# Three edits ahead of the main loop of a gated state-space layer: fp8 rounding by a step from the exponent bits, absolute maxima in one pass, the last gate store issued from the loop

## The chip, the cores and the metric

The program runs on one core of one Trainium2 chip. The metric is the device time of one execution in microseconds (us), the median of several runs. Engines are named PE (matrix unit), DVE (vector), ACT (scalar), POOL and SP (which here only issues transfers).

## The reference

x is 4 sequences of 1024 tokens of width 128. It is normalised (layernorm), run through a recurrent layer with 32 heads (`s`), and multiplied by a gate that comes from an fp8-rounded linear layer. What matters here is the gate:

```python
amax = jnp.max(jnp.abs(t))
scale = 448.0 / jnp.maximum(amax, 1e-12)
q = (t * scale).astype(jnp.float8_e4m3fn).astype(jnp.float32)
...
xq, wq = fake_quant_fp8(xn), fake_quant_fp8(weight)
g = silu(einsum('bsd,od->bso', xq, wq) + bias)
out = x + s * g
```

The largest absolute value is taken over the whole of x (and over the whole weight), so no token can be rounded before all are normalised.

## The kernel before

There are two parts, each a block of five instruction streams (one per engine) with semaphores between them. `prepare` does what is needed once: layernorm, transposes of the weights, cumulated angles and decays, and the gates. `units` then loops over 8 groups of 512 tokens (`t`, NS = 8) and 8 groups of 4 heads (`q`). No engine begins `units` before all have ended `prepare`. The order on each engine is the order of the code.

In `prepare`, tokens lie on the free axis of `xnT` (128 x 4096). DVE takes the largest and the smallest value of each quarter of it (`extreme`, L589). PE turns the result (L459), DVE makes the scales `sc` from it (L662 to L667), and ACT writes, for each t, the scaled numbers `fv` and their absolute values `fmag` (`gate_input`, L833). DVE rounds them in five passes over 512 columns (`quantise`, L687 to L693): fp8 by conversion at half size, a rounding by adding and taking off a large number for small values, and a choice between the two. PE multiplies the result with the rounded weight (L515) on top of the bias (`gate_bias`, L507). ACT applies Silu (L899) into `fgate`, a buffer of two halves, and SP stores that to DRAM (L270), the last step of `prepare` for it: it then waits until all gate stores have landed.

Between these steps of the gates, others are woven in: `log_part` on ACT (L888) with a subtraction on DVE (L737), and at t = 4 and 5 transposes on PE (L531), copies on ACT (L904) and after t = 5 three stores by SP (L274). `gate_input(t + 2)` waits until DVE has rounded t, Silu of t waits for PE, and from t = 2 on for the store of t - 2. `carry` belongs to `units`: its second half is first written at t = 1 of the loop.

Of the kernel before, what the change touches and what calls it, by code (L numbers as in the profile page):

```python
# [22 lines left out]
FP8 = mybir.dt.float8e4  # L23
# [4 lines left out]
P = 128  # L28
# [28 lines left out]
FP8_MAX = 448.0  # L57

# [32 lines left out]
def prepare(nc, K, dram, scratch, cum_stored, logs_stored, bc_loaded, xn_loaded):  # L91
# [3 lines left out]
    with ExitStack() as ctx:  # L95
# [49 lines left out]
        am, am2, sc = sb("a_am", [P, 2]), sb("a_am2", [2, 3]), sb("a_sc", [P, 7])  # L145
# [3 lines left out]
        half = sb("a_half", [P, ST], FP8)  # L149
        xq = sb("a_xq", [P, 2, ST], BF16)  # L150
        by_two = lambda a: tmp[:, a * ST:(a + 2) * ST].rearrange("p (i t) -> p i t", i=2)
        fv, fmag, fgate, small = by_two(0), by_two(2), by_two(4), tmp[:, 6 * ST:7 * ST]
# [31 lines left out]
        gate_stored = [sem("a_gate_stored0"), sem("a_gate_stored1")]  # L184
# [4 lines left out]
        def _(sp):  # L189
# [78 lines left out]
            for t in range(NS):  # L268
# [9 lines left out]
            for i in range(2):  # L278
                sp.wait_ge(gate_stored[i], 16 * NS // 2)
# [255 lines left out]
        def _(dve):  # L535
# [49 lines left out]
            peak = st32[:, 5, 0:2 * BATCH].rearrange("p (b i) -> p i b", i=2)  # L585

            def extreme(b, op):
                i = 0 if op == ALU.max else 1
                link(nc.vector.tensor_reduce(peak[:, i, b:b + 1], xnT[:, b * L:(b + 1) * L], AX.X, op))  # L589

            for g in range(0, 8, 2):
                dve.wait_ge(bc_squared, g + 1)
                nc.vector.tensor_copy(big[:, 512 * g:512 * g + 512], ps[B_BANK[g]][:]).then_inc(bc_copied_v, 1)
                extreme(g // 2, ALU.max)
# [23 lines left out]
            for i in range(BATCH):  # L618
# [8 lines left out]
            extreme(0, ALU.min)  # L627
            extreme(1, ALU.min)
# [10 lines left out]
            link(nc.vector.tensor_reduce(peak[:, 1, 0:1], peak[:, 1, :], AX.X, ALU.min))  # L639
            nc.vector.scalar_tensor_tensor(out=am[:, 0:1], in0=peak[:, 1, 0:1], scalar=-1.0, in1=peak[:, 0, 0:1],  # L640
                                           op0=ALU.mult, op1=ALU.max).then_inc(am_done, 1)
            wpeak = st32[:, 5, 2 * BATCH:2 * BATCH + 2]
            link(nc.vector.tensor_reduce(wpeak[:, 0:1], stage2[:, 10 * P:11 * P], AX.X, ALU.max))
            link(nc.vector.tensor_reduce(wpeak[:, 1:2], stage2[:, 10 * P:11 * P], AX.X, ALU.min))
# [966 lines left out]
```

## Time and profile before

| | |
|---|---|
| median of 3 runs | 1208.13 us (1207.28 to 1209.54) |
| the profiled execution | 1207.62 us, its span 1205.7 us |
| granted PE clock, mean of that execution | 0.971 |
| busy share of the span | PE 93%, DVE 95%, ACT 68%, POOL 63% |
| start of the first SP transfer of `units` | 137.25 us |

Times in a row are us from the start of the span. A timeline row gives start and length, engine, line, what is written and read, and in square brackets how long the engine was idle before it and who ended that. PEclk is the clock granted to PE as a share of full speed.

### The profile page before, as it was taken

The numbers are of one execution on the slowest core, as the hardware profiler recorded it, in microseconds if no ns is written. First come the engines' busy times: TensorE is split into PE (matmuls) and PEld (weight loads), VectorE is DVE, ScalarE is ACT, GpSimd is POOL, SyncE is SP. The second block draws the span as 40 slices with busy tenths as digits, with TensorE's granted clock in tenths as the row PEclk, the third lists the DMA queues.
The fourth block names the chain that finished last, engine by engine and source line by source line (L and its number), as shares of the span: only waits on it lengthen the run. The fifth ranks groups of instructions, "written<-read, shape, count | busy, mean of one in ns | idle before, by whom it ended". The sixth has DMA issues, their size and how long they took to land.

```text
span 1205.7 us, 30426 instructions
## 1 busy us (share of the span) xinstructions
PE 1124.8 (93%) x11442; PEld 817.4 (68%) x11442; DVE 1144.0 (95%) x1821; ACT 819.0 (68%) x1270; POOL 755.5 (63%) x560
## 2 busy tenths in 40 slices
PE   3878399999999999999999999999999999999996
PEld 3663267777777767777776777776777777777775
DVE  7899599999999999999999999999999999999994
ACT  4678366677676677667667776667767767777663
POOL 5000247776776767666776677776767687667774
PEclk9976699999999999999999999999999999999999
DMA  8654555544645465546555464546444655444450
GB/s 180 219 148 104 124 113 119 113 106 103 144 106 125 103 142 117 118 98 137 116 124 107 94 148 112 122 104 152 105 116 99 136 117 128 107 90 98 113 118 16
DMA packets 91888, 142.94 MB, mean 119 GB/s; under 512 B 19326, under 2 KB 38591, under 8 KB 91327
## 3 DMA queue, kind: packets, MB, share of 16 engines
q1 hardware_dynamic: 91743, 141.00, 50.5%
q8 instruction: 91, 1.49, 0.6%
q14 instruction: 54, 0.44, 0.1%
HBM read 58.68 MB, written 13.37 MB: 60 GB/s over the span
## 4 chain that ended last, share of the span: by engine, by line
PE 59%; DVE 17%; issue 7%; DMA 2%; ACT 1%; SPq 1%; POOL 0%; DVEq 0%; POOLq 0%; ACTq 0%
PE y L1235 10%; PE r L1221 8%; PE s L1138 7%; PE o L1153 6%; PE r L1112 5%; PE y L1229 5%; PE r L1118 5%; PE y L1245 5%; DVE hs L1373 3%; DVE M L1317 3%; DVE bw L1309 3%; PE r L1107 3%; DVE xc L1283 3%; PE r L1193 3%; PE d L1127 3%
## 5 line engine op out<-in xcount | busy, mean ns | idle before, releaser
L1524 POOL TENSOR_TENSOR rot<-part 128x512 f32<-128x512 f32 x256 | 384.1, 1500 | 315.9 <-DVE part L1299 315.9
L1299 DVE SCALAR_TENSOR_TENSOR part<-k_bcs,k_prmT,k_trig 128x512 f32<-128x512 f32 x512 | 524.8, 1072 | 13.5 <-issue 9.7
L1455 ACT ACTIVATE E<-d 128x512 f32<-128x512 f32 x256 | 152.9, 597 | 184.5 <-PE d L1127 184.2
L1533 POOL TENSOR_TENSOR ce<-rot,eb 128x512 f32<-128x512 f32 x128 | 185.8, 1471 | 2.3 <-POOLq L1563 2.1
L1317 DVE TENSOR_TENSOR M<-s,E 128x512 f32<-128x512 f32 x256 | 163.3, 676 | 2.0 <-PE s L1138 1.6
L1568 POOL TENSOR_TENSOR sqa<-sqa,sq 128x512 f32<-128x512 f32 x112 | 142.7, 1274 | 31.3 <-ACT sq L1465 22.7
L1112 PE MATMUL r<-k_w_zx,k_xns 128*128 128x256 f32 x512 | 137.0, 391 | 13.6 <-issue 9.4
L1138 PE MATMUL s<-rot 64*128 64x128 f32 x2048 | 149.4, 286 | 0.0
L1138 PEld LDWEIGHTS s<-rot 64*128 64x128 f32 x2048 | 124.9, 188 | 35.2 <-issue 34.8
L1460 ACT COPY xk<-r 128x512 f32<-128x512 f32 x128 | 75.3, 588 | 106.8 <-PE r L1112 106.6
L1235 PE MATMUL y<-M,xk 128*64 128x128 f32 x2048 | 140.1, 279 | 0.0
L1153 PEld LDWEIGHTS o<-k_w_o,yT 128*128 128x128 f32 x1024 | 132.8, 192 | 8.5 <-DVE yT L1409 1.7
L1221 PE MATMUL r<-k_xns,k_w_zx 128*128 128x512 f32 x256 | 133.2, 614 | 3.8 <-DVE xc L1283 1.8
L1153 PE MATMUL o<-k_w_o,yT 128*128 128x128 f32 x1024 | 133.4, 275 | 1.4 <-DVE yT L1409 1.4
L1235 PEld LDWEIGHTS y<-M,xk 128*64 128x64 f32 x2048 | 109.2, 136 | 21.5 <-issue 21.5
L1112 PEld LDWEIGHTS r<-k_w_zx,k_xns 128*128 128x128 f32 x512 | 90.5, 192 | 31.9 <-issue 11.0
L1127 PE MATMUL d<-k_cum,k_pick 123*128 123x512 bf16 x256 | 99.4, 388 | 0.0
L1502 ACT ACTIVATE sz<-r 128x512 f32<-128x512 f32 x128 | 75.7, 597 | 32.7 <-PE r L1221 32.1
L1283 DVE TENSOR_TENSOR xc<-r,k_cc 128x512 f32<-128x512 f32 x128 | 87.0, 680 | 4.8 <-ACT xk L1460 4.7
L1193 PEld LDWEIGHTS r<-xk,bw 128*64 128x64 f32 x1792 | 57.5, 137 | 48.8 <-DVE bw L1309 48.0
L1229 PEld LDWEIGHTS y<-k_ident,xc 128*128 128x128 f32 x512 | 58.8, 140 | 44.7 <-issue 44.7
L1409 DVE TENSOR_TENSOR yT<-y,sz 128x512 f32<-128x512 f32 x128 | 81.6, 676 | 6.3 <-PE y L1245 6.3
(253 smaller groups left out, 1676.3 us busy)
## 6 DMA issues: line engine op xcount, KB each, us to landing
k_trig<-k_tri SPq DMA_DIRECT2D x512, 128.0 KB, 2.4
eb<-ecum_rows SPq DMA_DIRECT2D x128, 256.0 KB, 4.7
k_bcs<-bc_t SPq DMA_DIRECT2D x16, 256.0 KB, 4.1
k_bcs<-bc_t SPq DMA_DIRECT2D x32, 128.0 KB, 4.2
k_bcs<-in_L_attn_u SPq DMA_DIRECT2D x4, 512.0 KB, 6.1
xn_t<-a_xnT SPq DMA_DIRECT2D x1, 2048.0 KB, 11.5
tc_t<-a_tcT SPq DMA_DIRECT2D x1, 2048.0 KB, 15.9
bc_t<-a_tmp SPq DMA_DIRECT2D x1, 2048.0 KB, 8.5
```

Source lines behind the costliest of these rows:

```text
L1112: last = nc.tensor.matmul(R[i][:, 256 * c:256 * c + 256], xns[:, (t + q // NQ) % 2, (2 * i + c) * P:(2 * i + c + 1) * P], K["w_zx"][:, DI ...
L1127: nc.tensor.matmul(Dp[:], K["pick"][:, head * P:head * P + P], K["cum"][0:D_ROWS, q % 2, h, :], start=True, stop=True).then_inc(d_ready, 1)
L1138: last = nc.tensor.matmul(Sp[j][:, k], rot[rows, q % 2, p, 0, k], rot[rows, q % 2, p, 1, k], start=True, stop=True)
L1153: last = nc.tensor.matmul(Op[:, k], yT[:, p, k], K["w_o"][:, (2 * q + p) * P:(2 * q + p + 1) * P], start=False, stop=q == NQ - 1 and c == ...
L1221: nc.tensor.matmul(R[p][:], w, xns[:, t % 2, :], start=True, stop=True).then_inc(z_ready, 1)
L1235: nc.tensor.matmul(Yp[p][m:m + 64, k], xk[:, par, c, 128 * p + m:128 * p + m + 64], M[:, 2 * p + j, k], start=False, stop=c == 0 and begin ...
L1299: nc.vector.scalar_tensor_tensor(out=part[:, 2 * p + f, :], in0=bcs[:, (t + q // NQ) % 2, 2 * w + f, :], scalar=col, in1=trig[:, p, 1 - f, ...
L1317: nc.vector.tensor_tensor(M[:, h, :], Sp[h % 2][:], E[:, h % 2, :], ALU.mult).then_inc(m_ready, 1)
L1455: nc.scalar.activation(E[:, h % 2, :], Dp[:], ACT.Exp).then_inc(e_ready, 1)
L1524: nc.gpsimd.tensor_tensor(rot[:, q % 2, p, w, :], part[:, 2 * p, :], part[:, 2 * p + 1, :], ALU.add).then_inc(rot_ready, 1)
L1533: nc.gpsimd.tensor_tensor(ce[:, p, :], rot[:, q % 2, p, 1, :], eb[:, p, :], ALU.mult).then_inc(ce_ready, 1)
L1568: nc.gpsimd.tensor_tensor(sqa[:], sqa[:], sq[:, p, :], ALU.add).then_inc(sqa_ready, 1)
```

## The change

Three edits. First, `quantise`: ACT now writes the number times its scale into `fv`, and the number times 2^20 times its scale into `ffar` (in place of the absolute value). DVE takes the exponent bits of `ffar` and sets the top bit of the mantissa (one pass over the bits as integers), which gives a number whose spacing is that of the fp8 grid. It adds the larger of this step and a least step to the number, and takes it off again. These are three passes for five. A second pair of scales (`sc[:, 6:8]`) is made in one more small DVE operation.

```diff
-            def quantise(dst, x, mg, m):
-                link(nc.vector.tensor_scalar(half[:, 0:m], x, 0.5, None, ALU.mult, saturate=False))
-                link(nc.vector.tensor_scalar(small[:, 0:m], x, 24576.0, -24576.0, ALU.add, ALU.add))
-                link(nc.vector.scalar_tensor_tensor(out=small[:, 0:m], in0=half[:, 0:m], scalar=-2.0, in1=small[:, 0:m],
-                                                    op0=ALU.mult, op1=ALU.add))
-                link(nc.vector.scalar_tensor_tensor(out=small[:, 0:m], in0=mg, scalar=2.0 ** -5, in1=small[:, 0:m],
-                                                    op0=ALU.is_lt, op1=ALU.mult))
-                nc.vector.scalar_tensor_tensor(out=dst, in0=half[:, 0:m], scalar=2.0, in1=small[:, 0:m],
-                                               op0=ALU.mult, op1=ALU.add).then_inc(xq_done, 1)
+            def quantise(dst, x, far, m):
+                step = small[:, 0:m]
+                link(nc.vector.tensor_scalar(step.bitcast(I32), far.bitcast(I32), EXPONENT, HALF_MORE,
+                                             ALU.bitwise_and, ALU.bitwise_or))
+                link(nc.vector.scalar_tensor_tensor(out=far, in0=step, scalar=STEP_LEAST, in1=x, op0=ALU.max, op1=ALU.add))
+                nc.vector.scalar_tensor_tensor(out=dst, in0=step, scalar=STEP_LEAST, in1=far,
+                                               op0=ALU.max, op1=ALU.subtract).then_inc(xq_done, 1)
...
+            link(nc.vector.tensor_scalar(sc[:, 6:8], sc[:, 0:2], FAR_UP, None, ALU.mult))
...
-                for dst, f in ((fv, ACT.Copy), (fmag, ACT.Abs)):
-                    nc.scalar.activation(dst[:, t % 2, :], xnT[:, t * ST:(t + 1) * ST], f, scale=sc[:, 0:1]).then_inc(x_scaled, 1)
+                for dst, k in ((fv, 0), (ffar, 6)):
+                    nc.scalar.activation(dst[:, t % 2, :], xnT[:, t * ST:(t + 1) * ST], ACT.Copy,
+                                         scale=sc[:, k:k + 1]).then_inc(x_scaled, 1)
```

Second, the maxima: the four reductions that sought a maximum now take it over absolute values, and the four that sought a minimum are gone, with the small operations that joined the two.

```diff
-                link(nc.vector.tensor_reduce(peak[:, i, b:b + 1], xnT[:, b * L:(b + 1) * L], AX.X, op))
+                link(nc.vector.tensor_reduce(peak[:, b:b + 1], xnT[:, b * L:(b + 1) * L], AX.X, ALU.max,
+                                             apply_absolute_value=True))
...
-            extreme(0, ALU.min)
-            extreme(1, ALU.min)
...
-            extreme(2, ALU.min)
-            extreme(3, ALU.min)
-            link(nc.vector.tensor_reduce(peak[:, 0, 0:1], peak[:, 0, :], AX.X, ALU.max))
...
+            nc.vector.tensor_reduce(am[:, 0:1], peak, AX.X, ALU.max).then_inc(am_done, 1)
```

Third, the last gate store: the gates lie in the second half of `carry`, which both parts share, so the store of the last one can be issued after `prepare`. SP issues it as its first transfer of `units`, no longer waits for gate stores at the end of `prepare`, and waits for them before it first loads gates (q = 5 of t = 0); DVE waits for them before it first writes that half of `carry` (t = 1, q = 0).

```diff
-            for t in range(NS):
+            for t in range(NS - 1):
                 sp.wait_ge(g_done, t + 1)
                 sp.dma_start(gate_d[t], fgate[:, t % 2, :]).then_inc(gate_stored[t % 2], 16)
...
-            for i in range(2):
-                sp.wait_ge(gate_stored[i], 16 * NS // 2)
...
+            sp.dma_start(gate_d[NS - 1], gate_kept(K)[:, (NS - 1) % 2, :]).then_inc(gate_stored[(NS - 1) % 2], 16)
             sp.dma_start(tcs[:, 0, :], tc_d[0]).then_inc(tc_loaded, 16)
...
+                    if t == 1 and q == 0:
+                        for i in range(2):
+                            dve.wait_ge(gate_stored[i], 16 * NS // 2)
```

On DVE, in `prepare`, between the last pass over the normalised B and C (`a_rowb` is a row of weights) and the chain that makes the decays (`a_s`), the order before was:

```order
L626 TENSOR_TENSOR a_rowb<-a_rowb 128x64
L589 TENSOR_REDUCE a_st<-a_xnT 128x1 [waits a_dch] x2
L631 TENSOR_TENSOR a_tcT<-k_bcs 128x2048 [waits a_bc_done,a_tc_stored,a_dch]
L634 SCALAR_TENSOR_TENSOR a_dl<-a_tcT,a_psx 128x512 [waits a_dch,a_rounded]
L589 TENSOR_REDUCE a_st<-a_xnT 128x1
L589 TENSOR_REDUCE a_st<-a_xnT 128x1 [waits a_dch]
L638 TENSOR_REDUCE a_st<-a_st 128x1 [waits a_dch]
L639 TENSOR_REDUCE a_st<-a_st 128x1 [waits a_dch]
L640 SCALAR_TENSOR_TENSOR a_am<-a_st 128x1 [waits a_dch]
L643 TENSOR_REDUCE a_st<-a_stage 128x1
L644 TENSOR_REDUCE a_st<-a_stage 128x1 [waits a_dch]
L645 SCALAR_TENSOR_TENSOR a_am<-a_st 128x1 [waits a_dch]
```

The same place in the changed kernel, on to the operation that waits for ACT (`a_inv_done`):

```order
L632 TENSOR_TENSOR a_rowb<-a_rowb 128x64
L635 TENSOR_TENSOR a_tcT<-k_bcs 128x2048 [waits a_bc_done,a_tc_stored,a_dch]
L638 SCALAR_TENSOR_TENSOR a_dl<-a_tcT,a_psx 128x512 [waits a_dch,a_rounded]
L640 TENSOR_REDUCE a_am<-a_st 128x1
L641 TENSOR_REDUCE a_am<-a_stage 128x1
L645 SCALAR_TENSOR_TENSOR a_s<-a_s 128x1024 [waits a_log_done,a_one_more]
L646 SCALAR_TENSOR_TENSOR a_s<-a_s,a_stage 128x1024 [waits a_dch]
L648 TENSOR_TENSOR a_s<-a_s,k_dec 128x1024 [waits a_inv_done,a_dch]
```

Four long reductions and four small operations have gone from in front of the scales and the decays.

On SP, from the gate stores to the first loads of `units` (the two branches are the end of one part and the start of the next), before:

```order
L270 DMA gate_rows<-a_tmp 128x512 [waits a_g_done] x6
L274 DMA log_parts<-a_cumT 32x32x128 [waits a_logT_out]
L274 DMA log_parts<-a_cumT 32x32x128 x2
L270 DMA gate_rows<-a_tmp 128x512 [waits a_g_done] x2
L95 UNCONDITIONAL_BRANCH [waits a_xn_stored,a_gate_stored1,a_tc_stored,a_gate_stored0,a_bc_stored,a_dup_stored,a_masks_stored]
L1008 UNCONDITIONAL_BRANCH [waits barrier_Pool_Activation_PE_DVE_SP_release]
L1049 DMA tcs<-tc_t 128x512
L1011 DMA k_pick<-cum_parts 12x4096 [waits logs_stored,cum_stored]
```

The same place in the changed kernel:

```order
L278 DMA gate_rows<-k_carry 128x512 [waits a_g_done] x6
L282 DMA log_parts<-a_cumT 32x32x128 [waits a_logT_out]
L282 DMA log_parts<-a_cumT 32x32x128 x2
L278 DMA gate_rows<-k_carry 128x512 [waits a_g_done]
L104 UNCONDITIONAL_BRANCH [waits a_tc_stored,a_xn_stored,a_bc_stored,a_dup_stored,a_masks_stored]
L1004 UNCONDITIONAL_BRANCH [waits barrier_Pool_Activation_PE_DVE_SP_release]
L1048 DMA gate_rows<-k_carry 128x512
L1049 DMA tcs<-tc_t 128x512
```

One gate store has moved behind the two branches, and the waits for the gate stores are no longer on the first of them.

## Rows read from the trace of the kernel before

**Rows 1.** Busy time by stretch: us, then each engine's busy time (instructions), PEclk, DMA

```profile
59.00:101.00 42.00, 31.37 (x161) 23.51 (x161) 39.87 (x57) 31.42 (x43) 2.35 (x1) 0.78 0.38 108
101.00:129.00 28.00, 22.80 (x82) 10.23 (x80) 25.58 (x43) 23.20 (x33) 0.00 (x0) 0.57 0.51 132
129.00:138.00 9.00, 0.31 (x3) 0.04 (x1) 0.00 (x0) 0.69 (x1) 0.00 (x0) 0.50 0.68 144
138.00:1205.00 1067.00, 1035.20 (x10948) 754.17 (x10948) 1031.33 (x1672) 729.89 (x1126) 737.66 (x518) 0.99 0.50 114
```

**Rows 2.** Timeline of DVE around the minima

```profile
63.46 2.48 DVE L589 TENSOR_REDUCE a_st<-a_xnT 128x1 f32<-128x1024 f32 x2
...
71.51 0.16 DVE L638 TENSOR_REDUCE a_st<-a_st 128x1 f32<-128x4 f32 x1
...
75.20 1.23 DVE L652 TENSOR_TENSOR a_s<-a_s,k_dec 128x1024 f32<-128x1024 f32 x1
```

**Rows 3.** Timeline of ACT at three places ahead of the gates

```profile
69.52 1.04 ACT L825 ACTIVATE a_s<-a_s 128x1024 f32<-128x1024 f32 x1
...
84.02 2.54 ACT L833 ACTIVATE a_tmp<-a_xnT,a_sc 128x512 f32<-128x512 f32 x4
...
95.12 0.69 ACT L872 ACTIVATE a_tcT<-a_ps,k_cols 128x512 f32<-128x512 f32 x1 [0.50 <-PE a_ps L481]
```

**Rows 4.** DMA issues of the page: count, KB each, us to landing

```profile
bc_t<-a_tmp SPq DMA_DIRECT2D x1, 2048.0 KB, 8.5
```

**Rows 5.** Busy time and granted clock of PE in three stretches: us, PE busy, PEclk

```profile
68.00:70.00 2.00, 0.64 (x6) 1.00 0.00 0
72.00:74.00 2.00, 1.18 (x7) 0.50 0.40 152
86.00:88.00 2.00, 0.01 (x1) 1.00 0.97 217
```

**Rows 6.** Timeline of PE after its two long waits, and in the gate loop

```profile
72.82 0.37 PE L459 MATMUL a_psx<-k_ident,a_am 128*2 128x128 f32 x1 [4.18 <-DVE a_am L645]
...
89.28 1.12 PE L473 MATMUL a_ps<-a_s,a_mats 128*128 128x512 f32 x2 [3.27 <-DVE a_s L676]
...
109.19 2.07 PE L507 MATMUL a_ps<-a_bias,k_ones 1*128 1x512 f32 x2
```

**Rows 7.** DVE from 101.05 to 128.7, by line: count, busy, mean ns, idle before

```profile
L689 DVE SCALAR_TENSOR_TENSOR a_tmp<-a_half,a_tmp 128x512 f32<-128x512 fp8e4 x8 | 5.5, 692 | 0.3
...
L687 DVE TENSOR_SCALAR a_half<-a_tmp 128x512 fp8e4<-128x512 f32 x8 | 3.4, 424 | 1.0 <-ACT a_tmp L833 0.8
```

**Rows 8.** ACT in the gate loop: us, ACT busy, PEclk, DMA share, GB/s

```profile
104.42:127.88 23.46, 19.20 (x28) 0.55 0.46 134
```

**Rows 9.** PE in the same stretch, same columns

```profile
104.42:127.88 23.46, 19.10 (x73) 0.55 0.46 134
```

**Rows 10.** Timeline of SP, whose rows are issues of transfers

```profile
72.31 0.36 SPq L248 DMA_DIRECT2D bc_t<-a_tmp  x1
...
127.91 2.31 SPq L274 DMA_DIRECT2D log_parts<-a_cumT  x3
130.68 2.88 SPq L270 DMA_DIRECT2D gate_rows<-a_tmp  x2
137.25 0.32 SPq L1049 DMA_DIRECT2D tcs<-tc_t  x1
```

**Rows 11.** Waits of SP: us in total, times, longest

```profile
SPq L1033 <- DVE part L1299: 4.4, 1, 4.4
...
SPq L281 <- DMA gate_rows<-a_tmp: 2.6, 1, 2.6
```

**Rows 12.** Tile a_tcT: the running sum on DVE, ns min/median/max

```profile
L577 DVE TENSOR_TENSOR_SCAN a_tcT<-k_ones,a_xnT x4: 2261/2264/2290, 29.9 to 36.4; 128x1024 f32<-128x1024 f32 x4
```

**Rows 13.** Timeline of DVE at the start of the loop, and its wait there for angles

```profile
138.36 3.75 DVE L1299 SCALAR_TENSOR_TENSOR part<-k_bcs,k_prmT,k_trig 128x512 f32<-128x512 f32 x4 [9.70 <-issue]
...
DVE part L1299 <- DMA k_trig<-k_tri: 3.2, 9, 0.5
```

More of the change, by code:

```diff
@@ L57 @@
 FP8_MAX = 448.0
+FAR_UP = 2.0 ** 20
+EXPONENT = 0x7F800000
+HALF_MORE = 0x00400000
+STEP_LEAST = 1.5 * 2.0 ** 14
 def bcast(ap, shape):
@@ L88, in load_bc, with gate_kept, prepare @@
             sp.dma_start(bcs[r:r + 32, t % 2, 1:4:2, :], src[32 * (1 - f):32 * (2 - f)]).then_inc(landed, 16)
-def prepare(nc, K, dram, scratch, cum_stored, logs_stored, bc_loaded, xn_loaded):
+def gate_kept(K):
+    return K["carry"][:, 1].rearrange("p k n -> p (k n)").rearrange("p (i t) -> p i t", i=2)
+def prepare(nc, K, dram, scratch, cum_stored, logs_stored, bc_loaded, xn_loaded, gate_stored):
     u, w_in, dt_bias, a_log, d_skip, b_norm, c_norm, b_bias, c_bias, norm_w, w_out, ffn_w, ffn_b = dram
@@ L148, in prepare @@
         bias4 = sb("a_bias4", [1, ST])
-        half = sb("a_half", [P, ST], FP8)
         xq = sb("a_xq", [P, 2, ST], BF16)
         by_two = lambda a: tmp[:, a * ST:(a + 2) * ST].rearrange("p (i t) -> p i t", i=2)
-        fv, fmag, fgate, small = by_two(0), by_two(2), by_two(4), tmp[:, 6 * ST:7 * ST]
+        fv, ffar, small = by_two(0), by_two(2), tmp[:, 6 * ST:7 * ST]
+        fgate = gate_kept(K)
         u_loaded = [sem(f"a_u_loaded{i}") for i in range(BATCH)]
@@ L731, in _ @@
                     dve.wait_ge(g_t, t - 1)
-                quantise(xq[:, t % 2, :], fv[:, t % 2, :], fmag[:, t % 2, :], ST)
+                quantise(xq[:, t % 2, :], fv[:, t % 2, :], ffar[:, t % 2, :], ST)
                 if t in (1, 3):
@@ L846, in _ @@
             act.wait_ge(sc_done, 2)
-            for i, f in enumerate((ACT.Copy, ACT.Abs)):
-                nc.scalar.activation(wv[:, i, :], w_ffn[:], f, scale=sc[:, 1:2]).then_inc(w_scaled, 1)
+            for i, k in enumerate((1, 7)):
+                nc.scalar.activation(wv[:, i, :], w_ffn[:], ACT.Copy, scale=sc[:, k:k + 1]).then_inc(w_scaled, 1)
             act.wait_ge(stored[2], 16)
@@ L905, in _, with units @@
                                        ps_bf[g % 2][0:3 * H].rearrange("p c t -> p (c t)")).then_inc(logT_out, 1)
-def units(nc, K, u, scratch, cum_stored, logs_stored, bc_loaded, xn_loaded, out):
+def units(nc, K, u, scratch, cum_stored, logs_stored, bc_loaded, xn_loaded, gate_stored, out):
     xn_d, tc_d, bc_d, cum_d, cumt_d, gate_d, logs_d, ecum_d = scratch
@@ L1039, in load_finish @@
                     sp.wait_ge(o_stored, 16 * t)
+                else:
+                    for i in range(2):
+                        sp.wait_ge(gate_stored[i], 16 * NS // 2)
                 sp.dma_start(gate[:], gate_d[t]).then_inc(gate_loaded, 16)
@@ L1382, in _ @@
                         angles(t, q + 2)
+                    if t == 1 and q == 0:
+                        for i in range(2):
+                            dve.wait_ge(gate_stored[i], 16 * NS // 2)
                     for c in range(CS):
@@ L1589, in program @@
         xn_loaded = ctx.enter_context(nc.semaphore("xn_loaded"))
-        prepare(nc, K, dram, scratch, cum_stored, logs_stored, bc_loaded, xn_loaded)
-        units(nc, K, dram[0], scratch, cum_stored, logs_stored, bc_loaded, xn_loaded, out)
+        gate_stored = [ctx.enter_context(nc.semaphore(f"gate_stored{i}")) for i in range(2)]
+        prepare(nc, K, dram, scratch, cum_stored, logs_stored, bc_loaded, xn_loaded, gate_stored)
+        units(nc, K, dram[0], scratch, cum_stored, logs_stored, bc_loaded, xn_loaded, gate_stored, out)
 NAMES = ["u", "in_proj_w", "dt_bias", "A_log", "D", "B_norm_w", "C_norm_w", "B_bias", "C_bias", "norm_w", "out_proj_w"]
```

22 lines of the change are left out of this document (7 added, 15 removed).

## The prediction

> **What bounds the kernel now.** I read busy time by stretch first [rows 1]. From 59 to 101 us DVE is busy for 39.9 of 42 us while PE and ACT each have some 10 us free: ahead of the gates, DVE sets the pace. From 101 to 129 us, the gate loop, DVE is busy for 25.6 of 28 us. From 129 to 138 us the engines do next to nothing; only transfers run. The rest, 1067 us, is the main loop, in which PE and DVE are both full; the change adds two waits and one transfer there and takes nothing out. So every gain must come from the first 138 us, and it must reach the start of the main loop, since `units` begins on all engines at once. DVE's first operation there is at 138.36 us [rows 13]; I work out how much sooner that comes.
>
> **A, ahead of the gate loop.** The minima are two pairs of 1024-column reductions, the first of them 2.48 us [rows 2], so 4.9 us for both pairs; of the small operations from 71.51 us on, some 0.7 us more go, since two remain of six. DVE would reach L652 at 75.20 - 5.6 = 69.6 us, but that one waits for ACT, whose L825 ends at 69.52 + 1.04 = 70.6 us [rows 3], and ACT does not move there, as it works without a wait on things that DVE had given it before the minima. So 4.6 of 5.6 us are left, and the added scale operation takes 0.2 (the size of those around it): 4.4 us at the scales. ACT's first gate inputs at 84.02 us [rows 3] need more than the scales: they overwrite the tile of the store `bc_t`, issued at 72.31 us [rows 10] and landing 8.5 us later [rows 4], at about 81 us. ACT gains 3.0 us there. After that ACT and DVE wait for each other by turns; DVE's lead of 4.4 us, and 0.6 us from the shorter rounding of the weight, help ACT to at most 3.7 us.
>
> PE takes some back. Its wait of 4.18 us before L459 goes (the maxima are ready before it asks), so it finishes its cumulated sums sooner and then waits longer for DVE before L473: 3.27 us now [rows 6], 2 to 5 us then. In the stretch in which the 4.18 us wait ends the clock granted was 0.50 (1.2 of 2.4 GHz), in the one in which it begins 1.00; in the wait of 3.27 us it stayed 1.00 [rows 5]. So either can happen. Two 512-column matmuls take 1.12 us at full clock and 2.07 us at half (L473 and L507) [rows 6]; four such pairs and six more matmuls stand between L473 and ACT's L872, which waits for PE already. I price a drop at 1.3 us: 2.4 us left of 3.7. I take **A = -3.0 us**, bounds -1.5 and -3.7.
>
> The Trainium skill, "TensorE: Matmul & The Clock Gate", section on the HAM clock gate, says that the clock falls to half when PE has been idle and comes back only after sustained work. By that rule the longer wait before L473 costs the 1.3 us; the trace agrees after one wait and not after the other.
>
> **B, the gate loop.** `quantise` of 512 columns is two operations of the kind L687 (0.42 us) and three of the kind L689 (0.69 us) [rows 7]. After, it is one integer operation with two immediates and two of the second kind. The trace has no bitwise operation. Bounds: 0.42 us, its nearest relation in form, and 0.69 us, if it ran like a two-tensor one. I take 0.43. With gaps a call falls from 3.1 to 1.9 us (2.2 by the upper bound). Eight calls save 9.6 us of DVE, but DVE then stops being the bound. From the first `log_part` to the last `log_parts` copy are 23.46 us, of which ACT is busy 19.2 [rows 8] and PE 19.1, at half clock [rows 9]. None of that work goes away; the two Copies with another scale cost what Copy and Abs cost (all of L833 is one price in the trace). So the loop can't take less than 19.2 us on ACT: 4.3 us is the most. ACT and PE hand over to each other: walking through the order with these durations, Silu of t = 1 stands behind four bias matmuls on PE (two pairs of 2.07 us), and the copies at t = 4 and 5 behind the bias for t = 7 and the transposes, for together some 2 us. The upper price of the bitwise operation adds at most 0.3 us, being behind ACT. I take **B = -2.2 us**, bounds -0.5 and -4.3. The lower bound is the case that SP's queue holds: Silu of t = 2 needs the store of t = 0 landed, which goes out behind the large stores of the decays.
>
> The Trainium skill, "VectorE: DVE Perf Modes", section on the perf-mode tier table, gives `tensor_scalar` on fp32 in SBUF two elements a cycle and two-tensor operations one. The trace agrees for the arithmetic ones (0.42 against 0.69 us). By that rule the bitwise operation is at its low bound, and the sum stays as it is.
>
> **C, the end of `prepare`.** After logT is copied, SP issues three log stores (127.91 us, 2.31 us), then two gate stores (130.68 us, 2.88 us, so until 133.56), then waits 2.6 us for landing [rows 10, 11], and its first issue of `units` is at 137.25 us. After, one gate store is left, half of 2.88 or 1.4 us less, and no landing is waited for: 1.4 + 2.6 = 4.0 us. The other engines are done by then: ACT is busy for only 0.69 us after 129 us [rows 1], with the last Silu, and it moves with the loop. **C = -4.0 us**; if the one store takes the whole of what the queue's backlog costs, -3.0.
>
> **D, given back in the main loop.** The store that moved comes ahead of the first loads: up to 1.4 us of SP. And SP then waits until the log stores have landed, which the 2.6 us had covered; the last went out by 127.91 + 2.31 = 130.2 us and had landed by the end of the wait at 136.2 us, in at most 6 us. With the log stores begun at time 0, SP's own work after them reaches its second transfer of `units` at about 5.6 us, and they land at 2.3 + 6 = 8.3 at the latest: the loads start up to 2.7 us later against the rest. Cover: after these loads SP now waits 4.4 us for DVE [rows 11] before it issues the next angles. Only from 4.4 us on would lateness show. The waits on `gate_stored` are for transfers issued a whole group of tokens earlier; behind DVE's wait stand the states of the loop, and it costs the handling of two waits. **D = +0.1 us**, upper bound +1.0.
>
> **The maxima.** An absolute maximum is not in the trace. Bounds: nothing, as the plain one (1.24 us), and the slowest operation of DVE on as many columns, the running sum with 2.26 us [rows 12], which is 4 x 1.0 us more. It would stand ahead of A and eat it. I take the lower one, since form and size are those of the reductions that are there.
>
> **Sum.** -3.0 - 2.2 - 4.0 + 0.1 = -9.1 us. The profiled execution took 1207.62 us, which gives 1198.5; its time is 0.5 us under the median of 1208.13, so against that I say 1199.0 us. This kernel's measurement can tell 0.2% (2.4 us) from no change.
>
> **Rivals.**
> 1. *ACT and PE run without a gap*: B at -4.3, A at -3.7, so -12 us: 1196. For it: the waits of ACT in the loop were waits for DVE. Against: PE's four bias matmuls at half clock. Chance 0.13.
> 2. *Another engine or queue takes DVE's place early*: the half clock ahead of L473, SP's backlog of stores, or slow absolute maxima leave A + B at -1 to -2 us; C stays. -3 to -7 us, 1201 to 1205. For it: `bc_t` and PE stand close behind DVE at each point of A. Against: these three would have to come to more than 3 us. Chance 0.18.
> 3. *No change that can be told*: all of that and a landing that SP still waits for, now of the log stores before its loads, beyond its cover of 4.4 us. 1206 to 1210. Against: SP's slack. Chance 0.05.
> 4. *Slower*: the first loads of the main loop are late, and so the angles (`k_trig`) stay late from one group of heads to the next. DVE waits for them already in 9 of the loop's rounds, 3.2 us in all [rows 13]. At 0.3 us in each of 64 rounds it would cost 19 us, +10 net: 1218. It decides from 9.1 / 64 = 0.14 us a round. Against: the SP queue waits for PE and DVE in every round, so a late start is worked off. Chance 0.04.
>
> **How the numbers follow.** The forecast (-7.5 to -10.5 us, 1197.6 to 1200.6) has 0.60. The range reaches to the whole of rival 1 (1195.9) and over the better part of rival 2 (1203.0); outside are 0.05 of rival 2 and rivals 3 and 4, with something for what I don't see, together under 0.2. Faster by over 0.2%: 0.60 + 0.13 + 0.18 = 0.91; within: 0.05; slower: 0.04.
>
> **What would show it.** DVE: no long reduction between 63 and 76 us, a wait for ACT before the operation that was L652, start of the first 512-column rounding near 98 us. ACT: first gate inputs near 81 us; in the gate loop ACT is nearly full and DVE waits for it. The bitwise operation at 0.43 us, the absolute maximum at 1.21 us. SP: no wait for gate stores, first issue of `units` near 128 us, DVE's first operation near 129.3 us; from there to the end the same time as before within 0.5 us. I am wrong if that last stretch grows, if the bitwise operation takes a microsecond or more, or if the first gate inputs do not come sooner than 83 us.

## The result, and the profile after

The changed kernel took 1198.75 us (median of 4 runs, 1196.45 to 1202.91), the kernel before 1208.31 us beside it: 0.9911 of its time, 95% interval 0.9881 to 0.994, or 9.6 us less. Measured once more it gave 0.9902 (0.9874 to 0.993). I had said 1199.0.

The kernel before ran beside each later batch too, at 1210.07, 1208.88 and 1209.99 us; most of its runs lie in two groups, near 1207 to 1210 and near 1214 to 1217, so that a median can move by a microsecond or two with the share of each.

The profiled execution was the slowest of the four: 1202.91 us, 4.7 us under the profiled one of before. Its span, read by stretch with the cuts at the same points of the program as in [rows 1] (us, then busy time of PE, PEld, DVE, ACT and POOL with instructions, PEclk, DMA share, GB/s):

```profile
59.00:98.00 39.00, 35.16 (x145) 26.59 (x145) 31.57 (x44) 28.02 (x39) 1.73 (x1) 0.63 0.42 120
98.00:124.00 26.00, 24.05 (x92) 11.47 (x92) 17.71 (x28) 23.76 (x34) 0.62 (x1) 0.57 0.52 132
124.00:130.00 6.00, 0.90 (x7) 0.36 (x5) 1.81 (x3) 3.49 (x5) 0.00 (x0) 0.50 0.57 115
130.00:1200.30 1070.30, 1034.98 (x10948) 753.99 (x10948) 1033.67 (x1672) 729.55 (x1126) 737.19 (x518) 0.99 0.50 114
```

DVE has 31.6 us of work in the first stretch instead of 39.9, and PE is now the full engine there, at a mean clock of 0.63 (before 0.78). In the gate loop DVE is busy for 17.7 us, not 25.6.

DVE at the places of [rows 2] and [rows 13] (start, duration, line, operation, idle before and what ended it):

```profile
66.63 0.15 DVE L640 TENSOR_REDUCE a_am<-a_st 128x1 f32<-128x4 f32 x1
...
69.47 1.23 DVE L645 SCALAR_TENSOR_TENSOR a_s<-a_s 128x1024 f32<-128x1024 f32 x1 [2.50 <-ACT a_stage L816]
...
73.36 1.23 DVE L648 TENSOR_TENSOR a_s<-a_s,k_dec 128x1024 f32<-128x1024 f32 x1 [1.41 <-ACT a_s L820]
...
82.12 0.16 DVE L658 TENSOR_SCALAR a_sc<-a_psx 128x2 f32<-128x2 f32 x1 [2.19 <-PE a_psx L469]
...
132.25 3.75 DVE L1299 SCALAR_TENSOR_TENSOR part<-k_bcs,k_prmT,k_trig 128x512 f32<-128x512 f32 x4 [6.33 <-SPq L1047]
```

The minima are gone, and what that frees comes back as waits: 2.50 and 1.41 us for ACT, 2.19 us for PE. The units begin at 132.25 us, 6.1 us sooner. ACT and PE in the same stretch:

```profile
63.06 0.69 ACT L808 ACTIVATE a_tcT<-a_psx,k_cols 128x512 f32<-128x512 f32 x1 [4.35 <-DMA tc_t<-a_tcT]
...
84.54 1.93 ACT L828 ACTIVATE a_tmp<-a_xnT,a_sc 128x512 f32<-128x512 f32 x3
```

```profile
59.46 3.67 PE L462 MATMUL a_ps<-k_ident,k_bcs 128*128 128x128 f32 x16 [4.23 <-DVE k_bcs L626]
...
74.62 6.87 PE L444 MATMUL a_ps<-a_cbT,a_tmp 128*128 128x32 f32 x32
81.43 0.58 PE L469 MATMUL a_psx<-a_am,k_ones 2*128 2x2 f32 x2
81.94 3.78 PE L473 MATMUL a_ps<-a_s,a_mats 128*128 128x512 f32 x4
...
89.81 1.12 PE L479 MATMUL a_ps<-a_s,a_mats 128*128 128x512 f32 x2 [1.15 <-DVE a_s L673]
```

DVE had the maxima at 66.97 us. PE, busy at half clock, still had the 32 small matmuls of L444 to work off before the two L469 that spread them; the scales followed at 82.12 us, and the first gate inputs stand at 84.54 us, not near 81. DVE in the gate loop by line (instructions | busy us, mean ns | idle before), to be held against [rows 7]:

```profile
L687 DVE SCALAR_TENSOR_TENSOR a_tmp<-a_tmp 128x512 f32<-128x512 f32 x7 | 4.8, 693 | 0.2
L688 DVE SCALAR_TENSOR_TENSOR a_xq<-a_tmp 128x512 bf16<-128x512 f32 x7 | 4.8, 692 | 0.2
L685 DVE TENSOR_SCALAR a_tmp<-a_tmp 128x512 int32<-128x512 int32 x7 | 3.0, 426 | 1.5 <-ACT a_tmp L828 1.3
```

And SP at the end of `prepare`, which answers to [rows 10]:

```profile
126.36 2.32 SPq L282 DMA_DIRECT2D log_parts<-a_cumT  x3
129.13 1.25 SPq L278 DMA_DIRECT2D gate_rows<-k_carry  x1
131.51 0.57 SPq L1048 DMA_DIRECT2D gate_rows<-k_carry  x1
132.13 0.44 SPq L1049 DMA_DIRECT2D tcs<-tc_t  x1
133.30 0.33 SPq L1007 DMA_DIRECT2D k_pick<-cum_parts  x1
133.68 0.35 SPq L1008 DMA_DIRECT2D k_pick<-log_parts  x1
```

There is no wait for the gate stores. The first issue of `units` is 5.15 us after the first log store, where it was 9.34 us.

Where the 4.7 us between the two profiles went, by marks in both traces (before, after): first `log_part` of the gate loop 104.42, 104.96: +0.5. From there to the first log store 23.49, 21.40: -2.1. From that to the first operation of `units` 10.45, 5.89: -4.6. From that to the end of the span 1067.34, 1068.75: +1.4. The section ahead of the loop gave nothing in this execution. What it gives in others is the question of the experiments.

### The profile page after: what moved, and what is told of

Read it like the earlier page. It is cut to its first block, busy times and chain, and to the rows that moved or that the text cites. A ratio compares the mean times of both kernels' runs of the same rounds, so it can differ in the third digit from the quotient of the medians.

```text
span 1201.0 us, 30402 instructions
## 1 busy us (share of the span) xinstructions
PE 1130.3 (94%) x11442; PEld 822.0 (68%) x11442; DVE 1131.8 (94%) x1796; ACT 818.6 (68%) x1270; POOL 755.2 (63%) x560
## 4 chain that ended last, share of the span: by engine, by line
PE 56%; DVE 19%; issue 8%; DMA 2%; ACT 1%; SPq 1%; POOL 0%; DVEq 0%; POOLq 0%; ACTq 0%
PE y L1235 10%; PE r L1221 8%; PE s L1138 6%; PE y L1229 5%; PE r L1118 5%; PE o L1153 5%; PE y L1245 5%; PE r L1112 4%; DVE M L1317 4%; DVE hs L1373 4%; DVE xc L1283 3%; DVE bw L1309 3%; PE r L1193 2%; PE r L1107 2%; PE d L1127 2%
## 5 line engine op out<-in xcount | busy, mean ns | idle before, releaser
L1299 DVE SCALAR_TENSOR_TENSOR part<-k_bcs,k_prmT,k_trig 128x512 f32<-128x512 f32 x512 | 527.1, 1077 | 9.2 <-SPq L1047 6.3
```

The lines of the kernel that those rows point to most:

```text
L1299: nc.vector.scalar_tensor_tensor(out=part[:, 2 * p + f, :], in0=bcs[:, (t + q // NQ) % 2, 2 * w + f, :], scalar=col, in1=trig[:, p, 1 - f, ...
```

## Experiments

**Theory.** The three edits add up. The first (maxima) gives 4 to 5 us ahead of the gate loop, if PE's clock is back at full before the maxima come; where it is not, PE takes DVE's place as the bound and the gain is lost. In the gate loop PE, with its bias matmuls at half clock, holds what the rounding could give. The end of `prepare` gives 4 us always. **Rivals:** ahead of the loop the order of the transfers decides (`tc_t` landed late and held ACT for 4.35 us); in the loop ACT alone or SP's queue does; at the end it is the landing alone, or the one issue less.

All profiles together, times in us. *B, C pass*: DVE begins the last pass over B and C; *inputs*: from there to ACT's first gate inputs (before 25.96); *next*: from there to the first `log_part`; *loop*: to the first log store; *end*: to the first operation of `units`; *main*: to the end of the span.

| kernel | median (range) | ratio (95%) | B, C pass | inputs | next | loop | end | main |
|---|---|---|---|---|---|---|---|---|
| before | 1208.31 | 1 | 58.06 | 25.96 | 20.40 | 23.49 | 10.45 | 1067.34 |
| after | 1198.75 | 0.9911 | 58.18 | 26.36 | 20.42 | 21.40 | 5.89 | 1068.75 |
| again | 1199.18 (1196.17-1202.62) | 0.9902 (0.9874-0.993) | 57.95 | 24.69 | 20.42 | 22.35 | 5.90 | 1068.09 |
| only_max | 1205.03 (1202.45-1211.1) | 0.9954 (0.9933-0.9975) | 57.67 | 21.70 | 19.99 | 23.48 | 10.07 | 1068.29 |
| only_round | 1209.93 (1204.48-1214.94) | 0.9995 (0.9974-1.0016) | 57.75 | 26.17 | 22.11 | 22.36 | 10.01 | 1070.60 |
| only_carry | 1206.35 (1203.63-1213.09) | 0.998 (0.9958-1.0003) | 57.38 | 25.97 | 22.12 | 22.97 | 6.25 | 1069.71 |
| warm1 | 1200.54 (1195.91-1205.0) | 0.9931 (0.9907-0.9954) | 63.33 | 20.88 | 20.26 | 22.36 | 5.90 | 1070.37 |
| tc_first | 1199.17 (1196.12-1205.57) | 0.992 (0.9895-0.9946) | 63.19 | 21.66 | 22.85 | 22.36 | 5.90 | 1067.74 |
| full_rows | 1197.71 (1196.03-1205.73) | 0.9914 (0.9889-0.994) | 63.87 | 21.99 | 22.67 | 20.38 | 5.55 | 1069.34 |
| no_bias | 1200.84 (1195.84-1204.77) | 0.9924 (0.9898-0.995) | 63.25 | 21.56 | 20.32 | 20.40 | 5.88 | 1070.09 |
| land_kept | 1201.54 (1199.62-1209.35) | 0.9926 (0.9898-0.9954) | 57.57 | 22.41 | 19.85 | 20.81 | 9.29 | 1068.27 |
| warm12 | 1199.18 (1197.49-1202.59) | 0.9903 (0.987-0.9937) | 57.88 | 20.83 | 21.42 | 20.69 | 5.89 | 1069.49 |
| combo2 | 1196.40 (1195.55-1202.02) | 0.9881 (0.985-0.9911) | 57.80 | 20.87 | 21.37 | 19.93 | 5.54 | 1069.09 |
| before_warm1 | 1208.68 (1206.89-1215.93) | 0.999 (0.9964-1.0015) | 57.34 | 26.64 | 20.41 | 23.47 | 10.43 | 1068.31 |

### The changed kernel again, and each edit alone

`again` is the changed kernel, unaltered.

> The changed kernel once more. Its first profile lost all of term A (the first gate inputs of ACT began at 84.54 us, not at 81), since ACT waited 4.35 us for the landing of the store tc_t and PE ran at half clock from there on. Theory 1 (A is there, but the landing of tc_t and PE's clock take it away in some executions): in this profile the first gate inputs begin anywhere from 81 to 84.5 us, and the sooner tc_t lands the sooner they begin; the median is 1196 to 1200 us with a spread of some 5 us, more than the 2 us of the kernel before. Theory 2 (A is never there, another wait behind it always takes it): first gate inputs at 84 to 84.5 us whatever tc_t does, median 1200 to 1203 us. Both: the stretch from the first log_part to the last log_parts copy 21.4 us, DVE's first operation of the loop 5.8 to 6.0 us after the log stores begin.

The other three are the kernel before with one edit each, taken from the diff above. only_max:

```diff
-                link(nc.vector.tensor_reduce(peak[:, i, b:b + 1], xnT[:, b * L:(b + 1) * L], AX.X, op))
+                link(nc.vector.tensor_reduce(peak[:, b:b + 1], xnT[:, b * L:(b + 1) * L], AX.X, ALU.max,
+                                             apply_absolute_value=True))
...
-            extreme(0, ALU.min)
-            extreme(1, ALU.min)
```

> The kernel before with the second edit alone (absolute maxima). Theory 1: DVE comes sooner to its chain, the gate inputs of ACT too unless tc_t lands late, and the DVE-bound gate loop starts and ends so much sooner: 0 to -3.5 us against the kernel before, about -2 in the median. Theory 2: DVE gains 5 us of work and loses them all in waits for ACT and PE: 0, within 0.5 us. The absolute maximum costs 1.21 us, as the plain one.

only_round has the new `quantise`, its two scales and the two Copies of ACT that feed it:

```diff
-                link(nc.vector.tensor_scalar(half[:, 0:m], x, 0.5, None, ALU.mult, saturate=False))
...
+                link(nc.vector.tensor_scalar(step.bitcast(I32), far.bitcast(I32), EXPONENT, HALF_MORE,
+                                             ALU.bitwise_and, ALU.bitwise_or))
```

> The kernel before with the first edit alone (rounding in three passes). Both theories: the gate loop is then paced by ACT and PE, 21.4 us in place of 23.5 us from the first log_part to the last log_parts copy, and the log stores and all behind them come 2.1 us sooner: -2.1 us, with -1.5 to -2.7 allowed for the small pass over the weight. A rival by which DVE's work still counts (8 x 1.2 us) would give -5 or more.

only_carry has the gate rows in K's tile, the last store and the waits in `units`:

```diff
-            for t in range(NS):
+            for t in range(NS - 1):
...
-            for i in range(2):
-                sp.wait_ge(gate_stored[i], 16 * NS // 2)
```

> The kernel before with the third edit alone (gates in carry, last store issued in the loop). Term C of the prediction: -4.0 us, from one issue of 1.4 us and a landing of 2.6 us fewer in front of the loop; the first profile of the changed kernel showed 4.2 us less between the first log store and the first SP issue of the loop. Rival (the landing of the log stores, which SP now meets at once, delays the angles): -2 to -3 us, with the loop behind DVE's first operation 1 us or more longer than in the kernel before (1067.3 us).

Measured, by the ratios of a kernel time of some 1210 us: only_max -5.6 us, only_round -0.6 (its interval reaches from -3.1 to +1.9), only_carry -2.4 (-5.1 to +0.4), together -8.6, against -11.9 (-15.2 to -8.5) for all at once. They add up within their intervals. Against what I had expected, only_max gave more (-2, at most -3.5), and only_round and only_carry gave less in the median (-2.1 and -4.0), which their intervals do not exclude. The rival of only_carry (-2 to -3 us, with a main loop longer by 1 us or more) has its numbers too, -2.4 and 1069.71 us; but only_round, without that edit, has 1070.60, so the longer main loop does not speak for it. In only_max PE had its clock back, and its gate inputs waited for the store, as I had predicted of them. PE by stretches of 4 us (us, PE busy, PEclk, DMA share, GB/s), first only_max, then again:

```profile
58.00:62.00 4.00, 3.05 (x15) 0.50 0.00 0
62.00:66.00 4.00, 4.00 (x34) 0.85 0.00 0
66.00:70.00 4.00, 3.00 (x28) 1.00 0.00 0
```

```profile
58.00:62.00 4.00, 2.77 (x13) 0.50 0.00 0
62.00:66.00 4.00, 4.00 (x22) 0.50 0.00 0
66.00:70.00 4.00, 4.00 (x21) 0.50 0.00 0
70.00:74.00 4.00, 4.00 (x22) 0.50 0.01 4
74.00:78.00 4.00, 4.00 (x21) 0.50 0.94 337
78.00:82.00 4.00, 4.00 (x13) 0.50 1.06 302
```

```profile
79.37 2.56 ACT L824 ACTIVATE a_tmp<-a_xnT,a_sc 128x512 f32<-128x512 f32 x4 [0.33 <-DMA bc_t<-a_tmp]
```

```profile
80.22 0.16 DVE L658 TENSOR_SCALAR a_sc<-a_psx 128x2 f32<-128x2 f32 x1 [3.26 <-PE a_psx L469]
```

The last two fences are ACT of only_max and DVE of again, which waits 3.26 us for PE before it can make the scales; in only_max DVE does not wait there. PE has the same instructions and the same wait of 4.2 us ahead of this stretch in both; in the one the clock came back before the next wait, in the other not until past 82 us. The inputs stand 21.70 us behind the pass over B and C in the one and 24.69 in the other. In again, ACT met no wait for `tc_t` (4.35 us in after), and yet the gain was mostly absent, so a late `tc_t` is not needed for the loss; in land_kept (below) ACT waited 1.99 us for `tc_t`, the clock came back, and the inputs stand at 22.41 us, so a wait for it does not bring the loss either. The late store costs the other 1.7 us of after at the most.

### Ahead of the gates: the clock or the transfers

warm1 is the changed kernel with a filler: four 512-column matmuls whose result nobody reads, in the place of PE's wait before L462:

```diff
+            for i in range(4):
+                nc.tensor.matmul(ps_x[1][:], K["w_th"][:, 0:P], tcT[:, 0:ST], start=True, stop=True)
             for g in range(8):
```

> The changed kernel with four further 512-column matmuls on PE, whose result nobody reads, in its wait of 4.2 us for DVE near 55 us. In the profiles so far the clock fell to 0.50 in that wait and came back at 62.5 to 64 us in four kernels, and not before 84 us in the two profiles of the changed kernel; term A was then +0.5 and -1.4 us, against -5.1 us in the profile of the absolute maxima alone. Theory 1 (A hangs on the clock of PE between 59 and 84 us): the clock stays at 1.00 through 56 to 68 us, the first log_part (106.0 to 103.1 us in those profiles) begins at 99 to 101 us, the median is 1195 to 1197 us, 2 to 4 us below the changed kernel, and the spread shrinks. Rival (A hangs on the landing of tc_t and bc_t): no change in the median beyond 1 us.

tc_first issues the stores of `xn_t` and `tc_t` ahead of the mask stores on SP:

```diff
             cum = K["cum"][:].rearrange("r b h t -> r (b h) t")
+            sp.wait_ge(xT_out, 8)
+            sp.dma_start(xn_d.rearrange("s p t -> p s t"), by_super(xnT)).then_inc(stored[0], 16)
+            sp.wait_ge(tc_done, BATCH)
+            sp.dma_start(tc_d.rearrange("s p t -> p s t"), by_super(tcT)).then_inc(stored[1], 16)
             sp.wait_ge(masks, 1)
```

> The changed kernel with SP's stores of xn_t and tc_t issued ahead of the seven fills of the mask tables. tc_t then lands by 55 us, so ACT does not wait for it at 58.6 us. Theory 1 (clock of PE): it takes away the 2.0 to 4.35 us wait of ACT there where it occurs, but if PE stays at half clock the gate inputs still begin at 82 us or later: median 0 to -1.5 us against the changed kernel. Rival (landings decide A): -2 to -4 us and first gate inputs at 81 us or sooner.

before_warm1 is the kernel before with warm1's four matmuls alone.

> The kernel before with the idle matmuls of warm1. Theory: in it PE waits for the maxima from 68.6 to 72.8 us whatever its clock is before that, and the clock falls in this wait, so a clock that stays up through 60 us gives nothing: 0, within 1 us, and 25.5 to 26.2 us from DVE's last pass over B and C to the first gate inputs. Rival (the gain of A is a matter of the clock at 60 us, not of the minima): -3 us or more here too.

warm12 is warm1 and four more of them in the wait before L479:

```diff
+            pe.wait_ge(turned, 1)
+            for i in range(4):
+                nc.tensor.matmul(ps_x[0][:], K["w_th"][:, 0:P], tcT[:, 0:ST], start=True, stop=True)
             pe.wait_ge(lin_taken, 2)
```

> The changed kernel with the idle matmuls of warm1 and four more of the same kind on PE in its second wait, before the shifted sums (L479). From the beginning of DVE's last pass over B and C to the first gate inputs the profiles show 21 to 22 us with PE's clock back at 62 to 67 us, 24.7 and 26.4 us with it at half until 84 us; from there to the first log_part 20.0 to 20.4 us, and 22.1 to 22.9 us in those four in which the clock fell in the second wait. Theory (these two falls of the clock decide what reaches the gate loop): 20.9 to 21.7 us and 20.0 to 20.4 us here, both at once, so 1 to 3 us below the changed kernel in the median. Rival (the fill-in matmuls delay PE as much as the clock gives back): no change.

PE in warm1. Its pass over B and C began 5.4 us later than in again, so the last two rows lie in the work that ran at 0.50 in again:

```profile
62.00:66.00 4.00, 3.42 (x15) 1.00 0.00 0
66.00:70.00 4.00, 3.96 (x36) 1.00 0.00 0
70.00:74.00 4.00, 3.39 (x32) 1.00 0.01 4
```

With the first filler the inputs stand 20.83 to 20.88 us behind the pass in all three profiles that have it (warm1, warm12, combo2). Without it, seven profiles with the new maxima lie at 21.56 to 22.41 (clock back early, five of them), 24.69 and 26.36 (not back). The four without the new maxima lie at 25.96 to 26.64, with the filler too: in before_warm1 the clock was 1.00 up to 60 us, but PE then had to wait for ACT, which waited 4.83 us for `tc_t`, and fell to 0.50 until 84. Before itself had the clock back at 1.00 by 64 us and stands at 25.96, so an early clock without the new maxima gives nothing. That is the theory for A: the maxima give 4 to 5 us when PE is at full clock, 1.3 us or nothing when not. One part of it is argued and not shown: no kernel held the clock down on purpose. The filler itself accounts for 0.7 to 1.6 us (20.83 to 20.88 against 21.56 to 22.41); that the clock makes the rest is read from executions with the same instructions. The rival was not tested by tc_first: in its batch all four profiles had no wait for `tc_t`, and its own 21.66 is like theirs. Its median is not told apart either. What speaks against the rival are again and land_kept, above.

In medians the filler bought nothing that shows (warm1 1200.54, warm12 1199.18, beside 1197.71 to 1200.84 of the others), where I had expected 1195 to 1197 us of warm1 and 1 to 3 us of warm12; the rival stated for warm12 is what came. For the second filler the profile says why. The clock was at 1.00 from 84 us to 96, but the filler itself ran too long:

```profile
79.23 2.59 PE L477 MATMUL a_ps<-a_s,a_mats 128*128 128x512 f32 x4
81.66 3.60 PE L480 MATMUL a_psx<-a_tcT,k_w_th 128*128 128x512 f32 x8
85.09 1.02 PE L484 MATMUL a_ps<-a_s,a_mats 128*128 128x512 f32 x2
```

ACT then waited 1.22 us for a matmul, and "next" is 21.4 us instead of 19.9 to 20.4. Where the clock fell in that wait, it is 22.1 to 22.9: in only_round, only_carry, tc_first and full_rows. Two of these have the old maxima, so this fall is not what the change brings.

### The gate loop: who holds it

full_rows turns each bias matmul from one row into 128 rows, of which 127 are zero (the weights pick row 0); what is computed stays the same:

```diff
-                nc.tensor.matmul(ps[2 + t % 4][:], ones[0:1, :], bias4[:], start=True, stop=False, skip_group_check=True)
+                nc.tensor.matmul(ps[2 + t % 4][:], row0[:], bias4[:], start=True, stop=False, skip_group_check=True)
```

> The changed kernel with the bias matmuls of the gate loop over 128 rows, of which 127 hold zeros, in place of one row; the result is the same. In every profile PE runs them at a granted clock of 0.50, 2.07 us a pair, and B (21.4 to 22.3 us for the stretch from the first log_part to the last log_parts copy) has gaps of ACT for PE. If the clock comes back with them, a pair takes 1.1 us and the stretch falls to ACT's own work, 19.2 to 20 us: -1.5 to -2.5 us against the changed kernel. If the clock stays at 0.50: 0. Rival to the PE part of B (ACT is held by the landing of gate stores): clock at 1.00 and yet 21.4 us or more.

no_bias leaves the bias of the gates out, to time the loop without these matmuls:

```diff
-                nc.tensor.matmul(ps[2 + t % 4][:], ones[0:1, :], bias4[:], start=True, stop=False, skip_group_check=True)
...
-                    last = nc.tensor.matmul(b[:, c * P:c * P + P], xq[:, t % 2, c * P:c * P + P], wq[:], start=False,
-                                            stop=c == CS - 1, skip_group_check=True)
+                    last = nc.tensor.matmul(b[:, c * P:c * P + P], xq[:, t % 2, c * P:c * P + P], wq[:], start=True,
+                                            stop=True, skip_group_check=True)
```

> The changed kernel without the bias matmuls of the gate loop (the bias is left out of the gates). PE then has 0.6 us of work for each t besides the transposes, at whatever clock. If PE's bias matmuls cause the gaps of ACT, the stretch from the first log_part to the last log_parts copy falls from 21.4 to 22.3 us to 19.2 to 20 us, and the median by 1.5 to 2.5 us. If it stays at 21 us or more, ACT waits for something else, the landed gate stores or the transposes.

The loop in tc_first (rows of the bias as they were), full_rows and no_bias, with the columns of the first fence:

```profile
107.70:130.06 22.36, 20.67 (x78) 9.40 (x76) 13.23 (x20) 19.22 (x28) 0.00 (x0) 0.50 0.49 141
```

```profile
108.53:128.91 20.38, 13.50 (x78) 6.80 (x76) 13.22 (x20) 19.11 (x28) 0.00 (x0) 0.88 0.53 155
```

```profile
105.13:125.53 20.40, 6.96 (x60) 5.50 (x60) 13.59 (x21) 19.06 (x28) 0.00 (x0) 0.58 0.53 154
```

PE was the bound: with the bias at 0.50 it is busy for 20.7 of 22.4 us. Take the bias away, and the loop takes 20.40 us, with ACT busy for 19.1. Keep all of it but over 128 rows, and the clock is at 0.88, the mean matmul of the line takes 0.80 us, not 1.12, and the loop takes the same 20.38 us. So the price of the half clock here is 2.0 us, and SP's queue, the same in all three, does not hold the loop. In medians full_rows is the lowest of its batch, but by less than its interval.

With the old bias the loop still takes 20.7 to 22.4 us, and what separates these is where PE stands when ACT begins its first `log_part`. PE of again, then of land_kept (the eight transposes ahead of the bias, and the second block of four bias matmuls):

```profile
98.69 1.94 PE L504 MATMUL a_ps<-k_ident,a_tcT 128*128 128x128 f32 x8 [1.78 <-issue]
...
104.81 3.78 PE L513 MATMUL a_ps<-a_bias,k_ones 1*128 1x512 f32 x4
```

```profile
95.47 1.06 PE L506 MATMUL a_ps<-k_ident,a_tcT 128*128 128x128 f32 x8 [1.79 <-issue]
...
100.03 3.78 PE L515 MATMUL a_ps<-a_bias,k_ones 1*128 1x512 f32 x4
```

From the start of this second block to the log stores it is 20.60 or 20.61 us in six of the seven profiles with the new rounding and the old bias, and 20.72 in warm12. The block begins 1.75 or 1.76 us after ACT's first `log_part` in again, only_round, warm1 and tc_first, 0.79 in after, 0.20 in land_kept, and 0.03 before it in warm12. In again the clock was down for the transposes already (1.94 us) and the first four bias matmuls took 3.77 us; in land_kept it fell only in these: 1.06 and 3.10 us. That is 1.55 us of PE, and the two loops differ by 1.54. With the old rounding it is the other way round: before, only_max and before_warm1 take 23.47 to 23.49 us from ACT's mark, though PE's block begins 0.53, 1.75 and 1.65 us after it; only_carry, with 22.97 us, fits neither.

### The end of prepare: landing or issue

land_kept is the changed kernel that waits at the end of `prepare` for the seven gate stores that are left there:

```diff
             sp.wait_ge(dup_stored, 2 * DUP)
+            sp.wait_ge(gate_stored[0], 16 * 4)
+            sp.wait_ge(gate_stored[1], 16 * 3)
```

> The changed kernel with SP waiting, at the end of prepare, for the landing of the seven gate stores issued there; only the issue of the last one stays in the loop. Splits term C, 4.2 us between the first log store and the start of the loop (10.0 to 10.45 us in kernels without the third edit, 5.9 us with it in four profiles). If both of its parts are there as the prediction had them, 1.4 us stay saved and 2.6 us come back: 8.0 to 8.8 us from the first log store to DVE's first operation of the loop, and +2.6 us in the median. If the landing is the whole of it, 10 us.

SP of land_kept, and its wait:

```profile
120.64 2.31 SPq L282 DMA_DIRECT2D log_parts<-a_cumT  x3
123.40 1.26 SPq L278 DMA_DIRECT2D gate_rows<-k_carry  x1
129.18 0.33 SPq L1050 DMA_DIRECT2D gate_rows<-k_carry  x1
```

```profile
SPq L289 <- DMA gate_rows<-k_carry: 3.4, 1, 3.4
```

The end is 9.29 us with the wait and 5.89 without: the landing is 3.4 us. Against the 10.45 of before, the one issue less is then 1.2 us (0.7 to 1.2 against the four kernels without the third edit). I had expected 8.0 to 8.8 us, and it is more, as the landing is longer than the 2.6 us of before. The median is 2.4 us above that of warm12, measured beside it (which has the fillers too), in the right direction, with intervals that overlap.

### All that helped, together

combo2 is the changed kernel with both fillers, tc_first's order and full_rows's bias; its edits are those shown.

> warm12 with the bias matmuls over 128 rows (full_rows) and the store of tc_t ahead of the mask fills (tc_first). The loop stretch should be 20.4 us as in full_rows, against 22.35 us in four of five profiles with bias matmuls over one row; both sections ahead of it as in warm12. 2 to 5 us below the changed kernel in the median, 1194 to 1197 us, the lowest of all; if the clock still falls ahead of PE's section from 28 us on, some runs 4 us longer.

It has the lowest median of all, 1196.40 us, and five of its six runs lie between 1195.55 and 1197.2. Against the kernel before it is 0.9881 (0.985 to 0.9911), against the changed kernel's 0.9902 (0.9874 to 0.993) the intervals overlap. That it is the faster is likely, not shown. Its profile has the shortest loop (19.93 us, ACT busy for 19.10) and the earliest start of `units`, 125.51 us.

## Why the prediction was right

**The prices of the operations held.** The absolute maximum of 1024 columns takes 1.21 us, what the plain one takes; the bitwise operation 0.426 us; a call of `quantise` 1.9 us. None of the upper bounds was needed.

**A, -3.0 with bounds -1.5 and -3.7, is the step that failed.** The steps on DVE and ACT were right, `bc_t` as the bound of the gate inputs too (only_max: 0.33 us of wait for it). But A is not one number. With the clock at full it is some -4.3 us (21.70 against 25.96; the three with the filler -5.1), beyond my upper bound: the store `bc_t` landed in 7.6 us and not 8.5, and was issued 14.1 us after the start of the pass, 0.1 us sooner than before. With the clock at half it is -1.3 (again) or +0.4 (after). I had asked what the longer wait before L473 does to the clock. There it could fall and cost more than the 1.3 us I set (some 2 us: 22.1 to 22.9 against 19.9 to 20.4), but it did so with and without the change. Neither the 1.3 us nor the 3.7 us from which I took it had a working of its own: the four pairs alone would lose 3.8 us by the durations I quoted (2.07 - 1.12 a pair), and I did not say what hides the rest. The place that decides was the other one: the wait of 4.2 us before the last transposes of B and C, which the change does not touch, and whose half clock DVE's minima had covered: in before, PE was ready and waited 4.18 us for the maxima [rows 6]. That the sum was within 1 us of the median may be because the executions mix both; only the profiled ones show which they were.

**B, -2.2, was too large in four profiles of seven.** I held ACT and PE together and came to the right mechanism, PE's four bias matmuls at half clock ahead of Silu; in those four it weighs 1.1 us more than I walked through. Of the kernels with the new rounding and the old bias, four took 22.35 or 22.36 us (-1.1) and three 20.69 to 21.40 (-2.1 to -2.8). PE is the bound in all seven, and its clock in the transposes and the first bias matmuls ahead of the loop decides which; of this I had said nothing. no_bias and full_rows show the 2.0 us that were there. The bound of -4.3 (ACT without a gap) nearly came in combo2: 19.93 us, or -3.6.

**C, -4.0, was right, its two halves less so.** -4.2 to -4.9 us in the profiles that have the edit in full; the landing is 3.4, not 2.6, and the issue 1.2, not 1.4, in sum 4.6 us. The profiles without the edit vary too, from 10.01 to 10.45 us; 10.45, from which I count, is the highest.

**D, +0.1, can't be told from what the main loop does anyway.** It takes 1067.3 to 1070.6 us in the 14 profiles, without a relation to the edits that shows: the ten with the third edit have 1069.1 us in the mean, the four without it 1068.6. Between before and after it grew by 1.4 us. I found no single cause: DVE's 512 operations of L1299 took 527.1 us together in place of 524.8; the longest of them is 1.84 us in after and 1.78 in before and in again. The rival of late angles did not come: DVE's waits for `k_trig` went from 3.2 us to 2.3. SP waited 0.7 us for the landing of the log stores, and had its slack behind it, as I had said of the cover: after the loads it next issues angles at 139.06 us, 3.1 us after the last load ahead of them.

**The total was right partly by luck**: B given too much in most profiles, C too little, A too narrow. Two of my own signs of being wrong came in the profiled execution: the first gate inputs at 84.54 us, not before 83, and a main loop longer by 1.4 us. The first was a true sign, of A. The second, "the same within 0.5 us", was wrong as a test, since the main loop varies by 3 us. And rival 2 did not add up as I wrote it: A + B at -1 to -2 with the whole of C is -5 to -6 us, not -3 to -7.

## What to carry to other kernels

Taking work off the busiest engine gives what the next one leaves, and the next may be a PE that was slow without anyone seeing, since the work removed had covered it: ask of each cover what clock the covered engine had. Here the edit that ended a wait for a landing (3.4 us with every engine idle) gave nearly the same in each profile (5.5 to 6.3 us in the nine that have it), and those that shorten work between two engines gave a spread (21.6 to 26.4 us ahead of the loop without a filler, 20.7 to 22.4 in it with the bias as it was). A stretch that is timed from one engine's mark moves with the place of the other engine at that mark: time it from the engine that bounds it. And take several profiles of the same program before a term of 2 or 3 us is read from one.

## What the runs showed of the hardware

The clock of PE was not settled by how long PE had worked. The Trainium skill, "TensorE: Matmul & The Clock Gate", section on the HAM clock gate, says that sustained work brings it back. In again PE was busy for 20.0 of 20 us from 62 to 82 us and stayed at 0.50, while only_max, with the same instructions on PE, was back at 1.00 from 66 to 70 us: the trace agrees with the page in the one and not in the other. The clock also fell with no wait ahead of it. In tc_first, as in the other three profiles of its batch:

```profile
28.00:32.00 4.00, 4.00 (x33) 1.00 0.77 267
32.00:36.00 4.00, 4.00 (x29) 0.73 0.94 340
36.00:40.00 4.00, 4.00 (x21) 0.50 0.93 337
```

where again kept 1.00 in all three stretches. These four began the pass over B and C some 5.4 us later (63.2 to 63.9, not 57.3 to 58.2). The profiled executions of tc_first and full_rows, with this fall, took 1205.57 and 1205.73 us, the other five of each 1196.03 to 1200.56 us. The four were measured on one chip, the other experiments on two others. As the other executions on that chip were short, the chip alone does not explain the time; whether they had the fall, only profiles could show. What brings about the one or the other stays open.

The second surprise was that zeros are worth multiplying: the gate loop with bias matmuls of one row ran at a mean clock of 0.50, with the same over 128 rows, 127 of them zeros, at 0.88, and PE was busy for 13.5 us instead of 20.7.
